# Two-layer graph attention: the adjacency in 1 MB transfers onto 128 partitions, x and node-row transfers of the first layer issued from GpSimd

## The reference

```python
h = jnp.maximum(_layernorm(x, axis=-1), 0.0)
x = x + L0(h, adj, W, b_W, a_vec, b_a)
h = jnp.maximum(_layernorm(x, axis=-1), 0.0)
x = x + L1(h, adj, W_w, W_b, a)
# one layer:
Wh = h @ W + b
e = leaky_relu((Wh @ a1)[:, None] + (Wh @ a2)[None, :], 0.2)
attention = softmax(where(adj > 0, e, -9e15), axis=1)
return attention @ Wh
```

## Time and profile before

| | us |
|---|---|
| median of 3 runs | 2206.73 |
| lowest, highest | 2205.22, 2226.64 |
| the profiled execution | 2236.48 |
| its span, first to last instruction | 2234.6 |
| mean granted clock of TensorE in it | 0.974 of full |

### The profile page before, as it was taken

One profiled execution on the slowest core, in us unless ns is written; L12 is line 12 of the kernel. 1 busy time (PEld: TensorE's weight loads), 2 busy tenths in 40 slices (PEclk: granted clock), 3 DMA queues, 4 the chain that ended last, 5 costly groups with the idle time before them and its releaser, 6 DMA issues.

```text
span 2234.6 us, 49031 instructions
## 1 busy us (share of the span) xinstructions
PE 2001.2 (90%) x16866; PEld 1698.2 (76%) x16866; DVE 1773.5 (79%) x2733; ACT 1139.9 (51%) x1097; POOL 318.6 (14%) x496
## 2 busy tenths in 40 slices
PE   5456889999988888899888879999999999999998
PEld 3234678887777777788777768888888888888887
DVE  6565778997777777789877678888888888888884
ACT  4455667886667677777777332222333333222331
POOL 6440112322111112222112300000000000000000
PEclk9997999999999999999999989999999999999999
DMA  5659999999999999999999650000000000000000
GB/s 140 167 138 231 258 273 297 339 277 271 269 265 256 259 269 275 283 303 286 279 271 277 176 108 29 28 28 28 28 27 27 28 28 28 28 28 28 28 28 9
DMA packets 117077, 357.46 MB, mean 160 GB/s; under 512 B 24624, under 2 KB 74032, under 8 KB 80176
## 3 DMA queue, kind: packets, MB, share of 16 engines
q1 hardware_dynamic: 114736, 340.23, 57.5%
q10 hardware_dynamic: 2304, 16.78, 1.9%
HBM read 314.84 MB, written 42.07 MB: 160 GB/s over the span
## 4 chain that ended last, share of the span: by engine, by line
PE 46%; DMA 37%; ACT 6%; SPq 4%; issue 3%; DVE 3%; DVEq 0%; POOL 0%; ACTq 0%; POOLq 0%
PE acc L541 45%; DMA adj_sb<-in_adj_dram 34%; ACT sign_a L603 5%; SPq L254 3%; DMA node_rows<-row_parts 2%; DMA mask_bytes<-pair_a 1%; DVE ext L793 0%; DVE masks L865 0%; ACT row_parts L591 0%; DMA masks<-in_x_dram 0%; PE ps_h L493 0%; SPq L280 0%; DVE row_parts L800 0%; DVE stats L713 0%; DVE centred L726 0%
## 5 line engine op out<-in xcount | busy, mean ns | idle before, releaser
L541 PE MATMUL acc<-node_rows,masks 128*128 128x258 f16 x16384 | 1888.4, 276 | 71.8 <-DVE masks L872 69.5
L541 PEld LDWEIGHTS acc<-node_rows,masks 128*128 128x128 fp8e4 x16384 | 1615.5, 99 | 325.6 <-issue 79.4
L603 ACT ACTIVATE sign_a<-adj_sb 128x2048 int8<-128x2048 int32 x256 | 489.1, 1910 | 285.0 <-DMA adj_sb<-in_adj_dram 284.2
L616 ACT ACTIVATE sign_z<-t_row,neg_s 128x2048 int8<-128x2048 f32 x256 | 504.4, 1996 | 2.0 <-DVE masks L865 1.9
L622 ACT ACTIVATE part_a<-acc,coef_a 128x258 f32<-128x258 f32 x128 | 60.2, 471 | 677.6 <-PE acc L541 677.6
L812 DVE TENSOR_SCALAR sign_z<-t_row,neg_s 128x2048 int8<-128x2048 f32 x256 | 326.9, 1278 | 2.9 <-issue 2.4
L872 DVE TENSOR_SCALAR masks<-masks 128x2048 uint32<-128x2048 uint32 x256 | 311.6, 1217 | 0.3
L865 DVE STREAM_TRANSPOSE masks<-sign_z 128x2048 uint32<-128x2048 uint32 x128 | 294.9, 2304 | 0.1
L892 DVE SCALAR_TENSOR_TENSOR part_ac<-acc,coef_c,part_a 128x258 f32<-128x258 f32 x128 | 61.9, 484 | 238.3 <-ACT part_a L622 238.3
L438 POOL TENSOR_TENSOR h_sum<-h_sum,ext 128x128 f32<-128x128 f32 x126 | 113.2, 898 | 736.9 <-DVE ext L793 733.3
L493 PE MATMUL ps_h<-w_ext,centred_t 128*128 128x133 f32 x256 | 80.9, 409 | 119.1 <-ACT centred_t L578 115.6
(11 more groups left out here) (83 smaller groups left out, 612.9 us busy)
## 6 DMA issues: line engine op xcount, KB each, us to landing
adj_sb<-in_adj_dram SPq DMA_DIRECT2D x1024, 256.0 KB, 11.1
node_rows<-row_parts SPq DMA_DIRECT2D x128, 129.0 KB, 9.2
node_rows<-node_rows SPq DMA_DIRECT2D x32, 516.0 KB, 12.3
mask_bytes<-pair_a ACTq DMA_DIRECT2D x16, 1024.0 KB, 10.8
pair_a<-mask_bytes SPq DMA_DIRECT2D x16, 1024.0 KB, 4.8
x_old<-in_x_dram SPq DMA_DIRECT2D x64, 64.0 KB, 12.6
x_after_layer<-x_new SPq DMA_DIRECT2D x64, 64.0 KB, 13.1
x_old<-x_after_layer SPq DMA_DIRECT2D x64, 64.0 KB, 1.8
```

The source lines that it names most:

```text
L541: mm = pe.matmul(acc[T.p][s][:, 0:ROW], stationary[s][:, c // BYTES, c % BYTES, :], node_rows[:, c, ROW * s:ROW * (s + 1)], start=(c == 0) ...
L603: nc.scalar.activation(sign_a[:, T.p, SPAN * r:SPAN * (r + 1)], adj_sb[:, r, :], ACT.Sign, scale=-1.0) \
L616: nc.scalar.activation(sign_z[:, T.p, SPAN * r:SPAN * (r + 1)], t_row[:], ACT.Sign, scale=-1.0, bias=neg_s[:, ds(RGROUPS * T.t + r, 1)]).t ...
```

## The change

`load_adj` issues one transfer per slot: all 128 partitions of slot r, with the source written as quarter x row x column. ScalarE's wait counts 16 per tile in place of 64. `load_x_old` and `store_x_new` of layer 0 and `store_rows` of the nodes of layer 1 leave SyncE's program; GpSimd's has them now, behind its power of the same tile: the store of `x_new` of tile T, the load of `x_old` of tile T+2, and the store of the node rows of tile T-1. In layer 1 and in the node phase the stores stay with SyncE.

```diff
--- before.py
+++ after.py
@@ -63,7 +63,6 @@
 HEAD = 4
 TAIL = 60
 NODE_STEP = 4
-QUAD_ORDER = (0, 2, 1, 3)
 
 
 class Tile:
@@ -249,11 +248,10 @@
         @block.sync
         def _(sp):
             def load_adj(T, r):
-                for a in QUAD_ORDER:
-                    sp.nop(nofuse=True)
-                    sp.dma_start(adj_sb[QROWS * a:QROWS * (a + 1), r, :],
-                                 adj[ds(T.t * TILE + QROWS * r, QROWS), SPAN * a:SPAN * (a + 1)]) \
-                      .then_inc(adj_loaded[r], 16)
+                sp.nop(nofuse=True)
+                sp.dma_start(adj_sb[:, r, :],
+                             adj[ds(T.t * TILE + QROWS * r, QROWS), :].rearrange("i (a c) -> a i c", a=QUADS)) \
+                  .then_inc(adj_loaded[r], 16)
 
             def load_x_old(l, T):
                 if T.u is not None or T.k >= 2:
@@ -319,9 +317,6 @@
             load_quadrant(QUADS - 1)
 
 
-            load_x_old(0, Tile(0))
-            load_x_old(0, Tile(1))
-
             def load_pair(T):
 
                 T.wait_before(sp, S[1].edge_bits, 1)
@@ -333,28 +328,18 @@
                     for r in range(RGROUPS):
                         sp.wait_ge(cast_done, RGROUPS * T.t + r + 1)
                         load_adj(T.plus(1), r)
-                if T.plus(-3).exists:
-                    store_x_new(0, T.plus(-3))
-                    load_x_old(0, T.plus(-1))
-                if T.plus(-4).exists:
-                    store_rows(1, T.plus(-4))
 
             sweep(sp, layer_0_tile)
-            load_x_old(0, Tile(TILES - 1))
 
             def reload_rows(g):
                 for a in range(QUADS):
                     if (a, g) != (QUADS - 1, VGROUPS - 1):
                         load_rows(1, a, g)
 
-            store_rows(1, Tile(TILES - 4))
-            store_x_new(0, Tile(TILES - 3))
             for p in range(2):
                 sp.wait_ge(S[1].rows_stored[p], 16 * (TILES // 2 - PER_GROUP // 2))
             sp.wait_ge(rows_free, 1)
             reload_rows(0)
-            store_rows(1, Tile(TILES - 3))
-            store_x_new(0, Tile(TILES - 2))
             sp.wait_ge(pair_stored, 16 * TILES // PACK)
             load_pair(Tile(0))
             for g in range(1, VGROUPS - 1):
@@ -362,9 +347,6 @@
                 reload_rows(g)
             sp.wait_ge(S[0].tile_summed, TILES)
             reload_rows(VGROUPS - 1)
-            store_x_new(0, Tile(TILES - 1))
-            store_rows(1, Tile(TILES - 2))
-            store_rows(1, Tile(TILES - 1))
 
 
             for p in range(2):
@@ -448,8 +430,31 @@
                 pool.tensor_scalar(row_parts[:, slot, ROW:ROW + PART], ext[:, T.p, 0:PART], b_and_d[:, T.p, 1:2], 1.0,
                                    ALU.mult, ALU.mult).then_inc(S[l].high_d, 1)
 
+            def store_x_new(T):
+
+                pool.wait_ge(S[0].fin, FIN * (T.t + 1))
+                pool.nop(nofuse=True)
+                pool.dma_start(x1_dram[ds(T.t * TILE, TILE), :], x_new[:, T.p, :]).then_inc(S[0].x_stored[T.p], 16)
+
+            def load_x_old(T):
+
+                if T.u is not None or T.k >= 2:
+                    pool.wait_ge(S[0].fin, FIN * (T.t - 1))
+                pool.nop(nofuse=True)
+                pool.dma_start(x_old[:, T.p, :], x[ds(T.t * TILE, TILE), :]).then_inc(S[0].x_old[T.p], 16)
+
+            def store_rows(T):
+
+                pool.wait_ge(S[1].low, T.t + 1)
+                pool.nop(nofuse=True)
+                slot, _ = row_slot(1, T)
+                pool.dma_start(rows_dram[1][ds(T.t, 1), :, :].rearrange("o p r -> p (o r)"), row_parts[:, slot, :]) \
+                    .then_inc(S[1].rows_stored[slot], 16)
+
             for l in range(LAYERS):
                 if l:
+                    load_x_old(Tile(0))
+                    load_x_old(Tile(1))
                     pool.wait_ge(S[0].nat_ps, 1)
                     pool.wait_ge(S[0].coefs, 2)
                     pool.wait_ge(limits, n_limits)
@@ -460,11 +465,18 @@
                         build_picks()
                     if T.exists:
                         node_step(l, T)
+                    if l:
+                        store_x_new(T)
+                        if T.u is not None or T.k < TILES - 2:
+                            load_x_old(T.plus(2))
+                        if T.plus(-1).exists:
+                            store_rows(T.plus(-1))
                     rest = T.plus(l - 1)
                     if rest.exists:
                         node_rest(l, rest)
 
                 sweep(pool, body, trail=1 - l, step=[NODE_STEP, 2][l])
+            store_rows(Tile(TILES - 1))
 
 
         @block.tensor
@@ -599,7 +611,7 @@
                 if r == 0 and (T.u is not None or T.k >= 2):
                     act.wait_ge(S[0].edge_bits, T.t - 1)
                     act.wait_ge(packed, T.t - 1)
-                act.wait_ge(adj_loaded[r], 16 * QUADS * (T.t + 1))
+                act.wait_ge(adj_loaded[r], 16 * (T.t + 1))
                 nc.scalar.activation(sign_a[:, T.p, SPAN * r:SPAN * (r + 1)], adj_sb[:, r, :], ACT.Sign, scale=-1.0) \
                   .then_inc(cast_done, 1)
```

## The result

| | us |
|---|---|
| kernel after, median of 4 runs | 3799.06 (3795.96 to 3800.07) |
| kernel before, median of 4 runs beside it | 2214.66 (2205.22 to 2226.64) |
| ratio after / before | 1.715, 95% interval 1.704 to 1.725 |
| profiled execution of after: its time, its span | 3799.98, 3798.4 |
| mean granted clock of TensorE | 0.808 |

The change makes the kernel 71% slower. The forecast was "slower", with 5100 us in a range of 3690 to 6250. The direction and the range hold, but the value lies 1300 us too high; the first rival, four undisturbed engines, had 3762.

The account below looks back on a forecast made before the run. The prediction took layer 0's adjacency DMA as the bound, TensorE close behind. With four engines, 1151.6 us outside the loop plus 63 tiles of 63.2 us gave a 5133 us span, stated as 5100 us, range 3690 to 6250.

Parts of the forecast that it names:

- the first rival: Layer 0's adjacency loads on four engines at 26.1 GB/s each, 41.4 us a tile, 3762 us in all; chance 0.27.
- step 2: Adjacency transfer in layer 0: source outermost count 4 gives only four engines work, taken as 63.2 us a tile.
- the rate of one engine: Speed of each of four engines loading adjacency: bounded by 13.0 and 26.1 GB/s, taken as 17.1.
- the nearest row: The old adjacency transfers' own rate from 600 to 1200 us, 17.1 GB/s an engine, giving 63.2 us a tile.
- the fast end: Upper engine rate, from 8 KB packets of a 1 MB load onto 128 partitions: 26.1 GB/s, 41.4 us a tile.
- the slow row: Node rows reloaded onto 32 partitions at a time, 1284 to 1290 us: 13.0 GB/s an engine, 83.2 us a tile.
- Step 4: Before the loop, tile 0's adjacency transfers delay node-row stores in SyncE's queue: 0 to 4 x 10 us, taken as 0.
- step 1: SyncE's adjacency issues fall from 1024 to 256; the saving counts as nothing under a busy DMA.
- step 3: x loads, x stores and node-row stores on GpSimd: at most 1.4 us an issue, 4.2 us a tile, hidden, taken as 0.
- step 5: Tail behind the last cast: TensorE's backlog gone but clock perhaps halved; taken as 0, within 15 us either way.
- the undisturbed rate: Four engines loading layer 0's adjacency at 26.1 GB/s each, 41.4 us a tile, 3762 us; chance 0.27.
- the middle: Four-engine outcome around the forecast value of 5100 us, from 4300 to 5900 us; chance 0.38.

Follow-up runs that it names:

- outer2: Kernel after with each slot loaded by two transfers of 64 partitions, source outermost count 2; 6310.38 us (one execution).
- outer128: Kernel after with the 1 MB source written with outermost count 128, rows landing on other partitions (attention wrongly placed); 2082.23 us, ratio to before 0.943.
- one_mb_only: Kernel before with only the single 1 MB adjacency transfer per slot, everything else still on SyncE; 3800.48 us, ratio to before 1.721.
- pool_only: Kernel after with four transfers of 32 partitions again, leaving only the move of loads and stores to GpSimd; 2232.06 us, ratio to before 1.011.
- one_at_a_time: Kernel after with SyncE issuing each 1 MB transfer only when the one before has landed; 5968.70 us, ratio to before 2.705.
- pool_adj: Kernel before with the 1 MB adjacency transfers (source count 4) of tiles 1 to 63 issued from GpSimd; 2968.56 us, ratio to before 1.355.
- gather_adj: Kernel before with 1 MB adjacency transfers of tiles 1 to 63 from GpSimd as indirect transfers, one index per partition; 2165.59 us, ratio to before 0.983.
- two_rings: Kernel before with quarters 0 and 1 of each slot issued from SyncE, quarters 2 and 3 from ScalarE; 2277.76 us, ratio to before 1.031.

## Why the prediction was right, and where it was wrong

- The shape of the transfer (step 2), on which all was to hang, is right. The DMA share fell from 1.03 to 0.28, and outer2, outer128 and one_mb_only show that the outermost count does it, and pool_only that the moved queues add about 1%. The range took in both ends of the rate of one engine, and so it held although the value was 1300 us off.
- The term that failed is the rate of one engine, in the same step: 17.1 GB/s taken "by the nearest row", 26.3 measured, 22 us a tile and 1395 us in all. The nearest row was the wrong one. The adjacency's 17.1 was measured with sixteen engines writing 32 partitions, the very thing that the change ends. I argued that the pairs of engines start each transfer together, and gave that weight against the fast end. Together they are only for some 20 us at the start of the loop: three transfers wait in each engine's queue, so an engine goes on to its next one without waiting for the others. The prediction counted the queue as full, "so yes", and did not ask what a full queue does to the phase of the engines. With that step the fast end, 41.4 us a tile, would have been the value; 41.06 was measured. The reason given for the factor of two between the two ends is not shown by its rows either: the slow row has packets under 8 KB only, the fast one none.
- Step 4, tile 0's transfers among the node-row stores, was bounded by 40 us and taken as 0. It is 61.8 us, outside its bound. The text named 10 to 16 us for each transfer and then bounded four of them by 10. Even 16 is short for one whose engines start together. By the packets in the trace of the kernel after, the first and the last of the four took some 27 and 25 us and the two in the middle 34 us together, with 606 ns as the median of their 8 KB packets; the four row slots cover part of that. That the term is tile 0's is shown; how much of each transfer's time is its own engines' and how much the node rows' beside it is not.
- Issue time (step 1) is worth nothing, as said: each issue is even held for 3.9 us in the median now, and still hides.
- GpSimd's issues (step 3) were bounded by 1.4 us each and cost 0.55 to 0.63 (1000 to 2600 us):

```profile
L437 POOL DMA_DIRECT2D x_after_layer<-x_new x39 | 24.4, 626 | 0.0
...
L444 POOL DMA_DIRECT2D x_old<-in_x_dram x39 | 21.5, 552 | 2.2 <-issue 2.1
...
L451 POOL DMA_DIRECT2D node_rows<-row_parts x39 | 21.3, 547 | 0.1
```

  Hidden under a 41 us tile, as said. "Uncovered, against a 17 us tile, it would still fit" was nearly right: pool_only has +1.1%.
- TensorE's clock falls to 0.72 in layer 0, between long waits for data, and the products that then take longer are hidden, as said. The tail (step 5) came to 987.3 us against 988.9.
- The chances: 0.27 for the undisturbed rate was too little, 0.38 around the middle too much. A middle value between two states is likely only if the kernel mixes the two, and the engines of this one, once apart, stay so: 8 KB packets take 309 ns in the median from 600 to 1200 us.

The two errors, -1395 and +61.8 us, together with the 1.6 us of the tail make the difference of the span, 3798 against 5133.

## What to carry to other kernels

Before merging transfers, write down the outermost count of both sides as the instruction will have it: a source rearranged to "quarter, row, column" has 4 whatever its destination is, and four engines move 103 GB/s. Merge so that the 128 partitions stay outermost, or gather by an index per partition where the layout doesn't allow it. And when a rate must be guessed for engines that work side by side, ask whether anything makes them start together: with transfers waiting in the queue they part and run free.

## What the runs showed of the hardware that was not expected

- An engine's 8 KB packet takes 309 ns in the median with four engines apart, and some 606 ns where four engines that write partitions 32 apart have just started together. In the kernel after this ends within some 20 us; in one_at_a_time it comes back with each transfer; in pool_adj the median stays at 618. The Trainium skill (SBUF — State Buffer, "Door 1: The DMA port swizzle") has partitions 32 apart on one port, which could give this factor of two; no run here tests it, nor whether the cause lies in reading four pieces of one row at a time.
- The issuing engine is held while 1 MB transfers of four engines stand in its queue: up to 18.5 us in one adjacency issue on SyncE, and 13.2 us in a small x load behind them (one_mb_only).
- From GpSimd, transfers of outermost count 4 keep 12.3 engines busy; from SyncE, 3.9.
- An indirect transfer of 128 rows of 8 KB lands as fast as a plain one (5.3 us) and costs GpSimd 1.1 us to issue in the median, 2.8 at most (gather_adj).
- Left open: the 1% of pool_only, the 3% of two_rings, the slow packets of pool_adj, why the engines drift apart, and what holds the sixteen engines at 17 GB/s each when they write 32 partitions at a time, since the order of the quarters is worth only 2% of the kernel's time.
